# A soft mixture of experts after an attention: the transpose of the slot sums beside that of the next tile's x, and the last dispatch inside the contraction ahead of it

## The reference, cut to what matters

```python
logits = einsum('bnd,des->bnes', x_n, mu_n)              # 16 experts, 128 slots each
dispatch = softmax(logits, axis=1)                       # over the tokens
combine = softmax(logits.reshape(B, N, E * S), axis=-1)  # over all slots
slot_in = einsum('bnd,bnes->besd', x_ln, dispatch)
h = gelu(einsum('besd,edh->besh', slot_in, W1) + b1)
slot_out = einsum('besh,ehd->besd', h, W2) + b2
out = x + einsum('bsd,bns->bnd', slot_out.reshape(B, E * S, D), combine)
```

## Time and profile before

| what | value |
|---|---|
| median of 3 runs | 470.61 us (468.89 to 471.13) |
| the profiled execution | 469.91 us, its span 468.1 us |
| mean granted clock of PE | 0.985 |
| PE, DVE, ACT, POOL busy | 94%, 83%, 61%, 39% of the span |

### The profile page before, as it was taken

The page is one execution under the profiler, slowest core; times in us unless marked ns, Lnnn a source line. Parts: engine busy times, 40 slices in busy tenths (PEclk is TensorE's granted clock), DMA queues, the critical chain, the costliest instruction groups (busy, mean ns, idle before and its releaser), DMA issues.

```text
span 468.1 us, 12815 instructions
## 1 busy us (share of the span) xinstructions
PE 439.4 (94%) x4816; PEld 379.2 (81%) x4816; DVE 388.6 (83%) x857; ACT 285.1 (61%) x553; POOL 182.5 (39%) x322
## 2 busy tenths in 40 slices
PE   0479999999999999999999999999999999999996
PEld 0457788878887778888888988988988988988985
DVE  6688999999999987797887787787797797797775
ACT  3276778878888675546447447447447447447443
POOL 4379999379996441204202202202202202202100
PEclk9869999999999999999999999999999999999999
DMA  8940000000002000321322321421421421421430
GB/s 220 262 182 24 3 3 24 1 4 1 3 1 74 2 2 1 92 57 47 92 52 62 100 52 51 101 50 50 101 50 50 102 50 50 101 50 50 101 99 17
DMA packets 27815, 28.54 MB, mean 61 GB/s; under 512 B 10960, under 2 KB 19072, under 8 KB 27520
## 3 DMA queue, kind: packets, MB, share of 16 engines
q1 hardware_dynamic: 27392, 27.48, 22.2%
q10 hardware_dynamic: 384, 0.52, 0.5%
HBM read 9.11 MB, written 2.10 MB: 24 GB/s over the span
## 4 chain that ended last, share of the span: by engine, by line
PE 74%; DVE 13%; POOL 4%; SPq 3%; DMA 3%; issue 2%; ACT 1%; ACTq 0%; POOLq 0%; DVEq 0%
PE bank L1025 13%; PE bank L1027 12%; PE bank L1026 12%; PE bank L1242 10%; PE bank L1264 6%; PE bank L1122 5%; PE bank L1105 5%; PE bank L1085 3%; DMA xa<-in_x 2%; PE bank L1143 2%; SPq L293 2%; DVE mx L763 2%; DVE pT L904 2%; DVE pb L768 2%; DVE pb L932 1%
## 5 line engine op out<-in xcount | busy, mean ns | idle before, releaser
L904 DVE STREAM_TRANSPOSE pT<-eb 128x512 f32<-128x512 f32 x64 | 44.5, 700 | 37.9 <-ACT eb L618 35.1
L1242 PE MATMUL bank<-w_raw,eb 128*128 128x130 f32 x512 | 60.8, 276 | 1.3 <-DVE w_raw L895 1.3
L1242 PEld LDWEIGHTS bank<-w_raw,eb 128*128 128x128 f32 x512 | 58.5, 190 | 2.7 <-DVE w_raw L895 2.4
L629 ACT ACTIVATE pb<-pb 128x768 f32<-128x768 f32 (+1 forms) x48 | 37.2, 774 | 28.2 <-DVE pb L932 28.2
L1025 PE MATMUL bank<-mun_h,xlT_l 128*128 128x512 f32 x128 | 52.1, 407 | 0.0
L932 DVE TENSOR_TENSOR pb<-bank,rh 128x384 f32<-128x384 f32 x96 | 49.3, 513 | 3.3
L624 ACT CAST xlT_h<-bank 128x256 fp32r<-128x256 f32 x16 | 5.9, 372 | 75.7 <-PE bank L1214 75.7
L618 ACT ACTIVATE eb<-bank,nshift,rn 128x512 f32<-128x512 f32 x64 | 46.3, 777 | 7.7 <-PE bank L1027 7.6
L1027 PE MATMUL bank<-mun_h,xlT_h 128*128 128x512 f32 x128 | 50.5, 395 | 0.0
L1026 PE MATMUL bank<-mun_l,xlT_h 128*128 128x512 f32 x128 | 50.5, 394 | 0.0
L545 ACT COPY pT<-bank 128x512 f32<-128x512 f32 x64 | 37.8, 590 | 19.0 <-PE bank L1105 18.0
(11 more groups left out here) (159 smaller groups left out, 1152.1 us busy)
## 6 DMA issues: line engine op xcount, KB each, us to landing
mu_raw<-pT SPq DMA_DIRECT2D x248, 64.0 KB, 2.0
mu_raw<-in_L_ffn_mu SPq DMA_DIRECT2D x1, 2048.0 KB, 10.5
out<-w_raw SPq DMA_DIRECT2D x16, 128.0 KB, 1.9
xa<-in_x SPq DMA_DIRECT2D x1, 1536.0 KB, 10.2
w_raw<-in_L_ffn_W SPq DMA_DIRECT2D x2, 512.0 KB, 9.5
w_raw<-in_L_ffn_W SPq DMA_DIRECT2D x1, 1024.0 KB, 7.7
xa<-in_x SPq DMA_DIRECT2D x1, 512.0 KB, 3.5
ctile<-in_ctx SPq DMA_DIRECT2D x1, 512.0 KB, 5.1
```

Of the source, the lines that this page charges most:

```text
L904: v.transpose(eblk[:, :, 4 * c:4 * c + 4, :].rearrange("p m e j -> p e m j"), eb[:, 4 * c:4 * c + 4, :].rearrange("p e (m j) -> p e m j", ...
L1242: m = mm(bank[HB[i]][:, n * 2 * HC:(n + 1) * 2 * HC], eb[:, e, :], xw[:, e, :], start=True, stop=True)
```

## The change

The transpose of the slot sums of tile `s` moves from the front of the combination to the start of the step, between the two transposes of the next tile's x, and goes into columns 256 to 383 of bank 6. Its high half is cast by ACT right behind that of x, ahead of the gelus, and its low half is made by DVE right behind that of x, ahead of `hidden`. DVE waits for the cast of the sums before it reads x from that bank. The combination, which overwrites bank 6, now waits for `esT_ready`. Step 0 keeps the old order. On ACT, steps 0 and 1 are written out and the loop starts at step 2. At the end, `dispatch(15)` goes between the fourth and the fifth of the eight groups of `contract(14)`, and DVE's `finish(14)` goes from the start of step 15 to behind `hidden(15)`.

```diff
ACT
             def esT_high(t, b=7):
...
-                a.copy(esT[:], bank[b][0:96, 0:P]).then_inc(esT_split, 1)
+                a.copy(esT[:], bank[b][0:96, (DIM if b == 6 else 0):(DIM if b == 6 else 0) + P]).then_inc(esT_split, 1)
...
-            def ffn_step(s, p, last=False, sums=True):
+            def ffn_step(s, p, last=False, first=False, sums=True):
                 if not last:
                     xlT_high(s + 1)
+                    if not first:
+                        esT_high(s, 6)
                 gelus(s)
                 if not last:
                     slot_exps(s + 1, 1 - p)
-                    esT_high(s)
+                    if first:
+                        esT_high(s)
                 gT_high(s)
...
-            with act.Fori(0, TILES // 2 - 1) as i:
+            ffn_step(0, 0, first=True)
+            ffn_step(1, 1)
+            with act.Fori(1, TILES // 2 - 1) as i:
DVE
             def esT_low(t, b=7):
...
-                v.tensor_tensor(esT[64:96, :], bank[b][64:96, 0:P], esT[64:96, :].bitcast(F32),
+                c = DIM if b == 6 else 0
+                v.tensor_tensor(esT[64:96, :], bank[b][64:96, c:c + P], esT[64:96, :].bitcast(F32),
...
             def ffn_step(s, p, last=False, ahead=True, first=False):
-                if not first:
+                if not first and not last:
                     finish(s - 1, 1 - p)
                 if not last:
                     clamp(s + 1, 1 - p)
+                    if not first:
+                        dve.wait_ge(esT_split, s + 1)
                     xlT_copy(s + 1)
+                    if not first:
+                        esT_low(s, 6)
                 if last:
                     sum_e(s, 1)
                 hidden(s)
                 if last:
+                    finish(s - 1, 1 - p)
                     sum_e(s, 2)
...
                 gT_low(s, 0)
-                esT_low(s)
+                if first:
+                    esT_low(s)
                 gT_low(s, 1)
PE
-            def transpose_xl(t, p):
+            def transpose_xl(t, p, sums=False):
                 pe.wait_ge(xl_ready, t + 1)
-                for k in range(KD):
+                for k in range(KD - 1 if sums else KD):
                     m = nc.tensor.transpose(bank[6][:, k * P:(k + 1) * P], xl[:, p, k * P:(k + 1) * P], ident[:])
-                m.then_inc(xlT_filled, 1)
+                if sums:
+                    pe.wait_ge(es3_ready, t)
+                    nc.tensor.transpose(bank[6][0:96, DIM:DIM + P], es3[:], ident[:]).then_inc(esT_filled, 1)
+                    nc.tensor.transpose(bank[6][:, (KD - 1) * P:KD * P], xl[:, p, (KD - 1) * P:KD * P], ident[:])\
+                        .then_inc(xlT_filled, 1)
+                else:
+                    m.then_inc(xlT_filled, 1)
...
-            def combine(t, last):
-                if not last:
+            def combine(t, first, last):
+                if first:
                     transpose_es(t)
+                elif not last:
+                    pe.wait_ge(esT_ready, t + 1)
...
-            def contract(t, last):
+            def contract(t, last, part=range(EXPERTS // 2)):
...
-                for i in range(EXPERTS // 2):
+                for i in part:
...
-                m.then_inc(y_filled, 1)
+                if i == EXPERTS // 2 - 1:
+                    m.then_inc(y_filled, 1)
...
+            def ffn_step(s, p, last=False, first=False, late=False):
                 if not last:
-                    transpose_xl(s + 1, 1 - p)
-                dispatch(s)
+                    transpose_xl(s + 1, 1 - p, sums=not first)
+                    dispatch(s)
...
-                contract(s, last)
+                if late:
+                    contract(s, last, range(0, 4))
+                    dispatch(s + 1)
+                    contract(s, last, range(4, EXPERTS // 2))
+                else:
+                    contract(s, last)
...
-            ffn_step(TILES - 2, 0)
+            ffn_step(TILES - 2, 0, late=True)
             ffn_step(TILES - 1, 1, last=True)
```

## The result

The changed kernel takes 474.46 us (median of 4 runs, 473.01 to 474.94) against 469.75 us for the kernel before: a ratio of 1.0089, interval 1.0057 to 1.0121. By the medians it is slower by 4.7 us, outside the range of 468.9 to 473.2 and above the forecast of 471.0. The profiled execution took 474.54 us, with a span of 472.7 us against 468.1.

The account below looks back on a forecast made before the run. PE was taken as nearly the bound, with DVE sharing a closed chain over two steps. Loop +0.70 less 0.30 at the end gave +0.40, 471.0 us at the median's level; range 468.9 to 473.2.

Parts of the forecast that it names:

- The step that failed: At the moved sums' transpose on PE: its new wait for `es3_ready` should find it set, so costs nothing.
- the +0.40 forecast: Whole kernel: +0.70 us from six loop iterations less 0.30 at the end; bounds -0.9 to +1.4.
- the pair: Two consecutive loop steps, a closed chain between PE and DVE: 35.19 us against 35.07, +0.12.
- the end: Tiles 14 and 15: dispatch 1.13 us earlier, most of it lost to DVE's waits; gain 0.30, bounds 0 and 1.13.
- The slower rival: Start of each step: waits break up the transposes into slots of 0.20; 472.8 us in all, chance 0.14.
- B to hidden: From PE's first x transpose of an even step (B) to DVE's first reciprocal of `hidden`: 1.97 us against 1.31.
- The price of esT_low: DVE's low half of the transposed sums, now between xlT_copy and the reciprocal: 0.43 us, at least 0.20.
- Hidden to xw: From DVE's first reciprocal to its last xw copy: 15.93 us against 16.36, as esT_low's 0.43 leaves.
- PE's last term: From the start of the dispatch to the next even step's first x transpose: 17.24 us against 17.35, bounds 17.15 and 17.35.
- the signs: What the profile after should show, among it the dispatch's wait for `xw` in odd steps growing by a few tenths.
- The loop's: Six loop iterations of two steps each: +0.7 us, bounds +0.2 and +1.4.
- The unrolled ACT steps: ACT's written-out steps replacing the loop's first pass: same work, ACT idle at each step's start, cost nothing.

Follow-up runs that it names:

- the filler: Changed kernel with 18 matmuls of 512 columns that nobody reads, on PE in step 1 ahead of the wait for the sums: 472.59 us, ratio 1.0069.
- POOL's order changed: Changed kernel with POOL's wait for second moments and square roots of the last five tiles moved behind the affine part of tile 3: 470.13 us.

## Why the prediction was wrong, point by point

**The step that failed** is the sentence that the new wait for `es3_ready` "should find it set, since the sums of a tile are made in the step before". That is so for DVE's sums and for steps 2 to 14. It is not so in step 1, because the transpose does not wait for DVE but for POOL, and POOL is in order: ahead of `spread_sums(1)` it had the wait for the second moments. The wait that the prediction put at nothing was 4.33 us, and step 1 took 5.8 us more. What stands ahead of an instruction in each queue that a move makes it depend on has to be read for every step that is written out, and the prediction's rows are only of steps 12 and 13 and the end. With this wait removed the kernel takes 470.13 us, and with the old order in step 1 469.21, both inside the range of the forecast. That is no proof of its terms: the +0.40 forecast is less than the totals can show, and the expert part of these runs is 0.2 shorter than before, not longer, as the points on the pair and the end below explain.

**The slower rival** had a chance of 0.14 and the right sign, but another mechanism: broken-up transposes. They are not broken up; the three stand 0.11 us apart from start to start. The Trainium skill, "TensorE: Matmul & The Clock Gate", section "Part 4: PE-mode transpose", gives about 275 ns for a transpose in a kernel. The rows have 0.27 us too, as the duration of one; the distance between two is less than half of that, so as a slot the trace does not bear the figure out.

**The clock** was in no term. PE stood for 4.33 us. The work behind that began at a granted clock of 0.50, the level of 1.2 GHz, and was at 1.00, that of 2.4 GHz, by the end of the dispatch, 0.65 over the whole of it. It cost 2.1 us, 1.9 of them in the dispatch, shown by the filler. The Trainium skill, "TensorE: Matmul & The Clock Gate", section "Part 1: The HAM clock gate (the "warmup" mystery)", says that an idle array falls to half its clock and that activity gives it back. The trace agrees: 0.50 behind the idle time, and 1.00 all through where the filler took its place.

**B to hidden** was forecast 1.97 and measured 1.87, against 1.31 before. The term that is off is ACT's: its second cast starts 0.27 us after the first, ahead of the first one's end, where I had 0.39. xlT_copy comes 1.09 after B in place of 1.21. The price of esT_low in its new place is right: 374.21 - 373.43 = 0.78 from xlT_copy to the reciprocal, against the 0.33 + 0.43 forecast.

**Hidden to xw** was forecast 15.93 and measured 15.92. **PE's last term** was forecast 17.24 and measured 17.23: from the last matmul of the logits to the combination it was 0.43 us (411.24 to 411.67) and is 0.33 (381.59 to 381.92), so the old slot gave back 0.10, what the third transpose costs in front, and the other 0.10 stayed, as the prediction allowed for. **The pair** was forecast 35.19 and is 35.07, in the sum of terms as in the windows; 0.10 of the 0.12 is the term B to hidden. The dispatch's wait for `xw` in odd steps did not grow as the signs had it: the dispatch comes 0.07 later after B there than in even steps, where it was 0.08 before. **The loop's** +0.7 became -0.1: its six iterations, steps 2 to 13, take 210.60 us against 210.74. Step 2 is 0.5 shorter, half of that also without the wait (17.73 with POOL's order changed), for a reason that was not looked for, and step 3 is 0.3 longer (17.78 against 17.46); the last two pairs are equal.

**The unrolled ACT steps** cost nothing, as forecast: they are in all runs on top of the changed kernel, in which the loss goes, and step 0 takes 18.76 to 19.48 us in the profiles with them, 18.81 to 19.07 in those without.

**The end** was forecast to gain 0.30 and gained 0.7. Its lines after the change:

```profile
458.70 3.85 PE L1260 MATMUL bank<-w_raw,eb 128*128 128x130 f32 x32
...
464.12 0.48 DVE L958 SCALAR_TENSOR_TENSOR w_raw<-bank,rs,xa 128x256 f32<-128x256 f32 x1 [0.47 <-PE bank L1039]
464.52 1.27 DVE L918 TENSOR_REDUCE es<-eb 128x4 f32<-128x512 f32 x2
465.21 0.59 ACT L639 CAST gT_h<-bank 128x512 fp32r<-128x512 f32 x1 [0.90 <-PE bank L1284]
...
466.11 1.35 DVE L952 TENSOR_TENSOR gT_l<-bank,gT_h 128x512 fp32r<-128x512 f32 x2
```

From B of step 14 (442.48) the dispatch comes after 16.22 us, where it came after 17.42 (454.58 - 437.16): 1.20 earlier, 1.13 forecast. `finish` does wait for PE, 0.47, as forecast. The last sums to the first gT subtraction is 1.59 where I carried over the 1.82 of the earlier trace rows: that distance had held a wait for ACT's cast (over at 461.44, the subtraction at 461.47), which comes earlier now. So of the 0.7 the sums' earlier start is 0.45 (459.65 - 437.16 = 22.49 after B before, 464.52 - 442.48 = 22.04 now), forecast 0.26 to 0.33, and the shorter distance 0.23.

## What to carry to other kernels

An earlier place for an instruction is an earlier deadline for everything that feeds it, through each in-order queue on the way; here it was missed in a written-out first step, where set-up work shares one of those queues. Look up in the old trace when each input was there and when it was used, step by step: the difference is what a move may take. And an idle matrix engine can cost more than the wait: here 4.3 us of waiting cost 2.1 more in the matmuls behind it.

## What the runs showed of the hardware

That two engines, neither of them the bound alone, set a pace between them over two steps, was argued from four terms and shown by breaking it: with `hidden` at B + 1.32 the pairs went from 35.07 to 34.91, every step alike. Work that nobody reads, put into a wait of the matrix engine, kept its granted clock at 1.00 and gave back 2.1 us. ACT's second cast from one bank started 0.10 us ahead of the first one's end (373.13 against 372.86 + 0.37).
